# Attention's transposes and weighted values as pairs of 64-row tiles, with later transposes issued ahead

## The reference, cut to what matters

```python
# B=8 sequences of S=64 tokens, D=512, H=16 heads of HD=32, LK=1601 context rows
q = split(hidden @ q_w.T + q_b); k = split(context @ k_w.T + k_b); v = split(context @ v_w.T + v_b)
scores = einsum('bhqd,bhkd->bhqk', q, k) / sqrt(HD)
probs  = softmax(where(mask > 0, -inf, scores))
ctx    = einsum('bhqk,bhkd->bhqd', probs, v)        # weighted values
x = x + ctx ...  # then x + attn(layernorm(x)), x + experts(layernorm(x))
```

## Time and profile before

| what | value |
|---|---|
| median of 3 runs (lowest, highest) | 1251.3 us (1250.09, 1251.83) |
| span of the profiled execution, the time that the profile has of it | 1248.0 us |
| what lies between that span and the runs' median | 3.3 us |
| busy share of PE, DVE, ACT, POOL | 98%, 68%, 54%, 12% |
| mean granted TensorE clock | 0.999 of 2.4 GHz |
| one round of attention | 54.57 us, 16 times |

### The profile page before, as it was taken

How to read it: one execution, slowest core, us unless ns; L and a number is a source line. 1 busy time by engine, 2 the same in 40 slices (tenths; PEclk the granted TensorE clock), 3 DMA queues, 4 the chain that set the end, 5 groups by cost and what they waited for, 6 DMA issues and landing times.

```text
span 1248.0 us, 22257 instructions
## 1 busy us (share of the span) xinstructions
PE 1226.0 (98%) x8533; PEld 1150.7 (92%) x8533; DVE 844.3 (68%) x2213; ACT 676.0 (54%) x1202; POOL 147.5 (12%) x84
## 2 busy tenths in 40 slices
PE   7999999999999999999999999999999999999998
PEld 7899999999999999999999999999978889989996
DVE  6566656566665656666565666677689888877887
ACT  6455545645554564555456355435555666767673
POOL 0003101300310150031013003100012000000012
PEclk9999999999999999999999999999999999999999
DMA  8102200220220022022002202200326777777663
GB/s 297 38 1 91 82 2 1 99 73 1 91 82 1 1 97 76 1 91 81 2 1 99 74 1 91 96 2 1 109 71 240 259 235 269 235 245 259 228 220 129
DMA packets 61046, 126.97 MB, mean 102 GB/s; under 512 B 3644, under 2 KB 21192, under 8 KB 60824
## 3 DMA queue, kind: packets, MB, share of 16 engines
q1 hardware_dynamic: 58776, 118.97, 27.8%
q0 software_dynamic: 2176, 6.72, 1.6%
HBM read 120.01 MB, written 14.32 MB: 108 GB/s over the span
## 4 chain that ended last, share of the span: by engine, by line
PE 88%; DVE 7%; ACT 2%; issue 1%; DMA 1%; SPq 0%; ACTq 0%; DVEq 0%
PE ptp L877 25%; PE work L877 21%; PE pv L1033 7%; PE ptp L1017 7%; PE work L915 7%; PE work L1248 6%; PE work L1250 3%; PE ptp L1271 2%; PE ptp L1274 2%; PE ptp L1272 2%; PE ptp L1273 2%; PE ptp L1275 2%; DVE w_lo L1618 1%; PE work L884 1%; DVE w_lo L1624 1%; DVE pt L1530 1%
## 5 line engine op out<-in xcount | busy, mean ns | idle before, releaser
L877 PE MATMUL ptp<-vw_hi,cx_hi 128*128 128x256 f32 x832 | 241.8, 291 | 0.0
L877 PE MATMUL ptp<-vw_lo,cx_hi 128*128 128x256 f32 x832 | 235.4, 283 | 0.0
L877 PE MATMUL ptp<-vw_hi,cx_lo 128*128 128x256 f32 x832 | 235.3, 283 | 0.0
L540 POOL TENSOR_TENSOR cx_lo<-raw,cx_hi 128x1664 fp32r<-128x1664 f32 x28 | 106.3, 3795 | 669.9 <-ACT cx_hi L601 669.9
L877 PE MATMUL work<-cx_hi,kw_hi 128*128 128x400 f32 (+1 forms) x504 | 175.1, 347 | 0.8 <-DVE cx_lo L1432 0.7
L877 PEld LDWEIGHTS ptp<-vw_hi,cx_hi 128*128 128x128 f32 x832 | 159.2, 191 | 17.0 <-issue 17.0
L877 PE MATMUL work<-cx_hi,kw_lo 128*128 128x400 f32 (+1 forms) x504 | 173.7, 345 | 0.0
L877 PE MATMUL work<-cx_lo,kw_hi 128*128 128x400 f32 (+1 forms) x504 | 173.2, 344 | 0.0
L1530 DVE TENSOR_TENSOR pt<-ptp,pt 128x512 fp32r<-128x512 f32 (+1 forms) x224 | 141.0, 649 | 33.8 <-ACT pt L601 30.3
L877 PEld LDWEIGHTS ptp<-vw_hi,cx_lo 128*128 128x128 f32 x832 | 159.3, 191 | 0.0
L877 PEld LDWEIGHTS ptp<-vw_lo,cx_hi 128*128 128x128 f32 x832 | 159.2, 191 | 0.0
(11 more groups left out here) (291 smaller groups left out, 2371.8 us busy)
## 6 DMA issues: line engine op xcount, KB each, us to landing
w1raw<-in_w SPq DMA_DIRECT2D x32, 1024.0 KB, 5.0
w2raw<-in_w SPq DMA_DIRECT2D x32, 1024.0 KB, 6.2
raw<-in_ctxT SPq DMA_DIRECT2D x31, 832.0 KB, 6.2
pr<-in_mask SPq DMA_DIRECT2D x8, 800.5 KB, 4.3
xrow<-x_rows SPq DMA_DIRECT2D x7, 256.0 KB, 6.1
y_rows<-y_out_rows POOLq DMA_DIRECT2D x7, 256.0 KB, 2.6
xs<-in_x SPq DMA_DIRECT2D x1, 1024.0 KB, 9.2
qwraw<-in_qwT SPq DMA_DIRECT2D x1, 1024.0 KB, 7.8
```

What stands on the lines that cost most here:

```text
L540: pool.tensor_tensor(cx[1][:, :, sl], raw[:, k % 2], cx[0][:, :, sl].bitcast(F32), ALU.subtract).then_inc(c_lo, 1)
L877: last = pe.matmul(dst, lhs(i, c), rhs(j, c), start=(c == 0 and (i, j) == (0, 0)), stop=(c == n - 1 and (i, j) == (1, 0)))
```

## The change

Transposes and weighted values become pairs. Each 128x128 transpose becomes two transposes of 64 rows of probabilities into 64 columns each, in the two row halves of the array, and each writes a bank of its own, so that a block takes a pair of banks. Each 128-row weighted-value product becomes two of 64 context rows, one into bank `ptp2`, one into `pv`, for the same 256 columns; so the sums now lie in two banks, and the sums' end has four copies of 64 rows on ScalarE (L696, L697 before: two), four adds of 64 rows on VectorE (two before) and one add more of 128 x 256.

Eight banks become four pairs: 0 and 1 are the `work` banks 0, 1 and 2, 3; pair 2 is `ptp0` and `ptp1`; pair 3 is `ptp2` and `pv`, where the sums lie while a group is weighed. `PAIR_OF` says which block goes where. Blocks 0 and 1 share pair 3, and both must be read before W0 starts. Step `t` moves from behind k4 to right behind the last scores. In `w0` the order on TensorE is T2 T3 T4 W0 W1 T5 W2 T6 W3 T7 W4 T8 W5 W6, in `w1` T9 T10 W7 T11 W8 T12 W9 T13 W10 W11 W12 W13. T0 waits for v5's bank to be read, T3 and T4 for the last item in work banks 0, 1 and 2, 3 (k1 and k5), T11 for that in 0, 1 (k7), the others for the block that was in their pair. Keys get banks 0, 1, 2, 3, 2, 3 before `w0` and 0, 1 behind it. There are still three slots `pt`. In the last sequence's second round `t` comes behind the last scores too, and the query step moves between `w0` and `w1`; the sum bank of the last group is no longer a `work` bank.

The core of the diff (left out: the same renaming of arguments on ScalarE and VectorE, declarations of banks):

```diff
-        steps += e[2:3] + v[6:] + e[3:]
+        steps += t + e[2:3] + v[6:] + e[3:]
...
-            steps += k[:5]
-        steps += t + k[5:6] + w[:1] + k[6:] + w[1:]
+            steps += k[:6]
+        steps += w[:1] + k[6:] + w[1:]
...
+TURNED_BY = [2, TPH + 2, 2 * TPH]
+FIRST_TURNS = [(2, 3), (TPH + 2, TPH + 3)]
+NEXT_TURN = {0: 4, 2: 5, 3: 6, 4: 7, 5: 8, 8: 11, 9: 12, 10: 13}
+PAIR_OF = [3, 3, 2, 0, 1, 2, 0, 1, 2, 1, 2, 0, 1, 2]
...
+        def turned_block(j, units):
+            jj = j % (2 * TPH)
+            start = 2 * P if jj == 1 else 0
+            return pairs[PAIR_OF[jj]][:, :, start:start + units * S].rearrange("p a (u q) -> p a u q", q=S)
...
-            def fold(b, last, g):
+            def fold(b, g):
                 act.wait_ge(pt_used, NPT * b + TPH * (g + 1) + PTD)
...
-                act.activation(folded[0:2 * HD, :], sums[2 * HD:P, 0:2 * P], ACT.Copy)
-                act.activation(folded[2 * HD:P, :], sums[0:2 * HD, 2 * P:4 * P], ACT.Copy).then_inc(folded_done, 1)
+                act.wait_ge(att_rows, 4 * b + g)
+                for rows, others, cols in sum_parts():
+                    act.activation(folded[rows, 0], sums[0][rows, cols], ACT.Copy)
+                    ins = act.activation(folded[rows, 1], sums[0][others, cols], ACT.Copy)
+                ins.then_inc(folded_done, 1)
...
             def turn(b, last, j):
-                g, first = j // TPH, 2 * (j % TPH)
-                pe.wait_ge(pt_lo, NPT * b + pt_before(j))
-                if j % (2 * TPH) == 0:
-                    pe.wait_ge(w_free, count(b, last, ("v", g // 2, TPH - 1)))
+                g, jj, first = j // TPH, j % (2 * TPH), 2 * (j % TPH)
+                h, pair = g // 2, PAIR_OF[jj]
+                if jj == 0:
+                    pe.wait_ge(w_free, count(b, last, ("v", h, 5)))
+                    pe.wait_ge(pv_free, 4 * b + 2 * h + 1)
+                if jj == 2:
+                    pe.wait_ge(w_free, count(b, last, ("v", h, TPH - 1)))
+                if jj in (3, 4):
+                    pe.wait_ge(w_free, before_pair(b, last, pair, ("w", 2 * h, 0)))
+                elif jj == 11:
+                    pe.wait_ge(w_free, before_pair(b, last, pair, ("w", 2 * h + 1, 0)))
+                elif jj > 4:
+                    owner = max(i for i in range(jj) if PAIR_OF[i] == pair)
+                    pe.wait_ge(pt_lo, NPT * b + 2 * TPH * h + owner + 1 + PTD)
...
-                for n in range(min(2, KT - first)):
-                    for rt in range(2):
-                        ins = pe.transpose(ptp[j % PTD][:, (2 * n + rt) * P:(2 * n + rt + 1) * P],
-                                            pr[:, (2 * g + rt) % 4, (first + n) * P:(first + n + 1) * P], ident[:])
+                for u in range(units):
+                    n, rt = u // 2, u % 2
+                    for a in range(2):
+                        rows = slice(S * a, S * (a + 1))
+                        ins = pe.transpose(block[:, a, u], pr[rows, (2 * g + rt) % 4, (first + n) * P:(first + n + 1) * P],
+                                           ident[rows, rows])
...
-            def weigh(b, last, j):
+            def weigh(b, j):
...
                     for rt in range(2):
-                        ins = pe.matmul(sums[:, rt * 2 * P:(rt + 1) * 2 * P],
-                                         vv[:, kt, g % 2, rt].rearrange("p a d -> p (a d)"),
-                                         pt[:, j % PTD, n, rt].rearrange("p a d -> p (a d)"),
-                                         start=(kt == 0 and rt == 0), stop=(kt == KT - 1 and rt == 1))
+                        for a in range(2):
+                            rows = slice(S * a, S * (a + 1))
+                            ins = pe.matmul(sums[a][:, rt * 2 * P:(rt + 1) * 2 * P],
+                                            vv[rows, kt, g % 2, rt].rearrange("p a d -> p (a d)"),
+                                            pt[rows, j % PTD, n, rt].rearrange("p a d -> p (a d)"),
+                                            start=(kt == 0 and rt == 0), stop=(kt == KT - 1 and rt == 1))
...
             def weighted(b, last, g):
-                end = 2 * TPH * (g // 2 + 1)
-                for j in range(TPH * g, TPH * (g + 1)):
-                    if j + 2 < end:
-                        turn(b, last, j + 2)
-                    weigh(b, last, j)
+                base = 2 * TPH * (g // 2)
+                for jj in FIRST_TURNS[g % 2]:
+                    turn(b, last, base + jj)
+                for jj in range(TPH * (g % 2), TPH * (g % 2 + 1)):
+                    if jj in NEXT_TURN:
+                        turn(b, last, base + NEXT_TURN[jj])
+                    weigh(b, base + jj)
...
             def group_out(b, g):
...
+                for rows, others, cols in sum_parts():
+                    dve.tensor_tensor(folded[rows, 0], sums[1][rows, cols], folded[rows, 0], ALU.add)
+                    ins = dve.tensor_tensor(folded[rows, 1], sums[1][others, cols], folded[rows, 1], ALU.add)
                 ins.then_inc(pv_free, 1)
                 dve.wait_ge(pv_free, 4 * b + g + 2)
+                dve.tensor_tensor(summed, folded[:, 0], folded[:, 1], ALU.add).then_inc(sums_done, 1)
```

More of the change, by code:

```diff
@@ L165, in by_pair, with ring_banks, before_pair @@
     return [bank[:, 0:n * 2 * P].rearrange("p (n g r d) -> p n g r d", n=n, g=2, r=2)[:, :, :, rt, :] for rt in range(2)]
+def ring_banks(last):
+    banks, scored, others, late = [], 0, 0, False
+    for kind, a, j in STEPS[last]:
+        if kind == "s":
+            banks.append(scored % 4)
+            scored, others, late = scored + 1, 0, False
+        elif kind == "w":
+            others, late = 0, True
+        elif kind in "kanq":
+            plain = others % 4 if others < 4 or last else 2 + others % 2
+            banks.append(2 if last and (kind, j) == ("k", 5) else plain)
+            others += 1
+    return banks
+BANKS = [ring_banks(False), ring_banks(True)]
 def bank_of(last, step):
-    return step[2] % PTD if spare(step) else RING[last].index(step) % 4
+    return step[2] % PTD if spare(step) else BANKS[last][RING[last].index(step)]
 def before_bank(b, last, step):
     q = RING[last].index(step)
[L176 to L180, removed]
+    bank = BANKS[last][q]
+    mine = [m for m in range(q) if BANKS[last][m] == bank]
+    if mine:
+        return count(b, last, RING[last][mine[-1]])
+    other = max(m for m in range(len(RING[0])) if BANKS[0][m] == bank)
+    return NW * b + FIRST_K + max(ITEMS[0].index(RING[0][other]) + 1 - NW, bank - 3)
+def before_pair(b, last, pair, weighed):
+    earlier = STEPS[last][:STEPS[last].index(weighed)]
+    return count(b, last, [m for m in earlier if m in RING[last] and bank_of(last, m) // 2 == pair][-1])
 def pt_before(j):
@@ L377, in layer, with sum_parts, pt_part @@
         turn_banks = [work[1], work[2], yb[2], work[3]]
-        def sum_bank(last, g):
-            return work[3] if last and g == 3 else pv
+        def sum_parts():
+            halves = [slice(2 * HD * rt, 2 * HD * (rt + 1)) for rt in range(2)]
+            return [(halves[rt], halves[1 - rt], slice(rt * 2 * P, (rt + 1) * 2 * P)) for rt in range(2)]
+        def turned_block(j, units):
+            jj = j % (2 * TPH)
+            start = 2 * P if jj == 1 else 0
+            return pairs[PAIR_OF[jj]][:, :, start:start + units * S].rearrange("p a (u q) -> p a u q", q=S)
+        def pt_part(j, n, part):
+            return pt[:, j % PTD, 0:n, :, part, :].rearrange("p n r (a q) -> p a (n r) q", a=2)
         def scattered(ph, e):
```

73 lines of the change are left out of this document (33 added, 40 removed).

## The result

The changed kernel takes 1274.8 us (median of 4 runs, 1272.97 to 1276.46) against 1250.7 us for the kernel before beside it (1249.95 to 1251.83). The ratio is 1.0193, 95% interval 1.0179 to 1.0208: 1.9% slower. The forecast was 1270.

A forecast was written before the change was run, and what follows sets the result against it. TensorE, busy 98% of the span, was taken as the bound. 12.2 (15 rounds of +0.81) + 2.7 (mask rounds) + 4.5 (last round) = 19.4 us on 1248.0 gives 1267.4, with the median's 3.3 1270.7; forecast 1270, range 1246 to 1290.

The forecast's parts named there:

- the likeliest case: Whole kernel: slower, at 1270 us (its own range 1260 to 1280), through waits for banks; chance 0.57.
- Pairs of products cost one product: Weighted-value products on TensorE: a pair of 64-row products costs 0.12 us, like one 128-row product, no gain.
- A pair of transposes 0.062: Transposes on TensorE: a pair takes 0.062 us, saving 0.046 on each of 52, 2.4 us a round.
- Rival A: Transposes on TensorE don't get cheaper, 0.108 a pair: 17 us more, 1287; chance 0.15.
- Switches of 0.13 and 0.20: TensorE between 128-row and 64-row work: 0.13 us into a transpose, 0.20 back; 0.26 net a round.
- The waits: TensorE waiting for banks: T0 0.46 us, T4 0.94 (starts at 1.75), T6 0.37 (at 4.16), T11 0.75 (at 2.09).
- Rival B: T0, T4 and T11 find v5's, k5's and k7's banks free: no waits, about 1233 us; chance 0.2.
- Mask rounds: Seven rounds where VectorE converts the mask before the first scores: 0.39 us later each, +2.7 us.
- Rounds together: 15 rounds at +0.81 us (t +0.07, w0 +0.62, w1 +0.12), +12.2, plus 2.7 for rounds with a mask.
- The last round: Last sums, delayed by longer sums, row weights and query copy, ready at 912.6 instead of 908.1: +4.5 us.
- The step from span to runs: Whole kernel: the runs' median lies 3.3 us above the profiled span; carried along, 1267.4 becomes 1270.7.
- Rival C: Whole kernel: switches dearer or cheaper and waits half as long cancel, within 0.2% of before; chance 0.08.

The follow-up runs named there:

- the kernel with paired transposes alone: The changed kernel with only the transposes as 64-row pairs, products of 128 rows into one bank with short sums: 1283.2 us, ratio 1.0259 to the kernel before.
- all three later: The changed kernel with T4 behind W1, T11 behind W8 (T12 behind W9, T13 behind W10) and step t behind v6: 1257.2 us, ratio 1.0055.
- with the row weights moved: T4, T11 and t placed later in the changed kernel, plus last-round row weights behind the last turned blocks instead of the query copy: 1254.9 us, ratio 1.0035.
- the last pair of kernels: Sums handed over in halves and mask converted ahead of sums, added to the 1254.5 us kernel (rows later) and the 1254.9 us one (without): 1243.6 and 1243.3 us.
- the last kernel: The 1254.9 us kernel (turns later, row weights moved, without rows later) plus sums handed over in halves and mask ahead of sums: 1243.3 us, ratio 0.994.
- the other order: The changed kernel's own order, with short sums: 64-row tiles with half of the sums left out 1263.1 us, against 128-row tiles 1277.4 us.
- VectorE's rows are moved: The kernel before, with VectorE's four adds into the attention rows of a half's first group behind the second group's last block: 1250.9 us, ratio 1.000.
- whole tiles: The changed kernel's order, banks and waits, but transposes and products of 128 rows again and short sums: 1277.4 us, ratio 1.0213 to the kernel before.

## Why the prediction was right, and by how much it was off

*Direction and cause* were right, and it was the likeliest case that came. Point by point:

- *Pairs of products cost one product.* Eight products take 0.71 and sixteen 1.19, so a pair is (1.19 - 0.71) / 4 = 0.12: right.
- *A pair of transposes 0.062.* T0 and T1 together (sixteen) take 0.71, eight take 0.46: 0.0625 a pair. Rival A is out.
- *Switches of 0.13 and 0.20.* Two of them cost 0.28 in the kernel with paired transposes alone, where 0.33 was taken. The size is about right; which of the two is the dearer, that kernel does not tell.
- *The waits.* T0 0.41 (scores end 510.93, T0 at 511.34; forecast 0.46), T4 at 1.70 (1.75), T6 at 4.17 (4.16), T11 at 2.06 (2.09). Rival B, that these banks are free in time, is out: VectorE is idle for 1.57 us before k5's subtract, and T4 still starts 1.70 after k5's last product. w0 +0.68 (forecast +0.62), w1 +0.17 (+0.12).
- *Mask rounds.* 0.41 more than the others (0.39).
- *Rounds together.* 17.1 us, with the start's 0.6 apart, against 14.9 forecast. 0.11 a round is missing (1.7 in 15 rounds), which is the 0.06 of w0's term and the 0.05 of w1's; 0.3 more is the one mask round of 56.19, and the last 0.2 I did not follow.
- *The last round* is the term that was mis-sized: +4.5 forecast, 5.9 + 1.7 found. The chain was as described: T11 waits for the query copy behind sums and row weights (2.24), the last sums need 4.95 from W13's end (926.83, where a query product starts) to 931.78 (forecast 4.9). What I left out is the clock. Of the 3.1 us by which the term is short, T11 to W13's end is 1.0 and the query products are 1.7, both in slower stretches; the prediction had put the clock at nothing without a word.
- *The step from span to runs.* I carried 3.3 us from the profiled execution's span to the median. Every execution whose span is on record lies 1.7 to 1.9 above it; the rest of the 3.3 was that the profiled one was a fast one. After the change the median lies 0.2 above the profile's span, since its own execution (1276.46) was the slowest of the four. By the spans the change costs 26.6, by the medians 24.1; forecast 19.4. That the forecast comes within 4.7 of the median, and not within 7.2 as its 1267.4 does of the span of 1274.6, is luck.

Rival C, cancellation to within 0.2%, did not come either. Nearest to it are the kernels with the order mended: all three later is +0.55%, with the row weights moved +0.35%.

What the prediction did not see is how much of the loss could be had back. It had the longer sums in three of its terms (T11's later bank in w1, the mask rounds, the last round) but never added up their share. Without them 11.7 us are gone, nearly half of the loss; and the last pair of kernels, with the longer sums in place, is faster than the kernel before.

**Left open.** Whether the gain of the last kernel (7.4 us) belongs to the tiles: neither its order with 128-row tiles was run, nor the kernel before with its sums handed over in halves and its mask ahead of them. For the tiles speaks that in the other order they save 14.3 us with the sums kept short, that the kernel before has only 0.17 of wait in a round to lose and no longer rounds behind a mask, and that it gains nothing when VectorE's rows are moved. The two edits of the last pair, halves and mask, were run only together. Four slots for turned probabilities instead of three, which might free the last wait of w1 (0.25), were not tried.

## What to carry to other kernels

Before an instruction is issued earlier, look up when the bank that it writes is handed back, and count from the last product into that bank: here product, copy and subtract take 1.6 us, even with VectorE idle, and everything behind the early instruction on TensorE pays. Where a change splits an accumulation into two banks, the reader of these banks gets the bill; look for work of that engine that can stand where it waits anyway, and signal the copies in halves (the two together won 9.0 us by the spans, 11.5 by the medians). And before mixing tile heights inside a loop of short products, price the switches: here two for each block cost 0.28 us, twice what the cheaper transposes saved.

## What the runs showed that I had not expected

**The clock falls behind waits of the last round, and not in every execution.** Besides the trace after, most of the traces of kernels with 64-row products have one or two slower stretches, all in the last round; two have none. The same wait comes with both: 1.85 us for the copy of the hidden rows. The stretches around and behind it in the kernel with all three later and the row weights moved, where T4's products start at 890.57 (columns as above):

```profile
889.00:892.00 3.00, 1.70 (x32) 1.57 (x32) 2.38 (x5) 2.98 (x6) 0.00 (x0) 1.00 0.26 42
892.00:895.00 3.00, 2.73 (x55) 2.52 (x54) 2.39 (x5) 1.86 (x4) 0.00 (x0) 1.00 0.28 53
```

And in the last kernel, where they start at 881.80:

```profile
880.00:883.00 3.00, 1.47 (x22) 1.48 (x24) 2.38 (x5) 2.93 (x6) 0.00 (x0) 0.88 0.28 51
883.00:886.00 3.00, 3.00 (x42) 3.00 (x40) 1.74 (x3) 1.52 (x3) 0.00 (x0) 0.55 0.19 47
```

In the second the sixteen products behind the wait take 1.68 instead of 1.19, and the eight transposes 0.63 instead of 0.40. The same work up to the first group's last products takes 5.24 (881.80 to 887.04) instead of 4.38 (890.57 to 894.95), so this stretch costs 0.9 us on top of the wait. Waits of 0.7 to 1.0 us inside the rounds never did this: the stretches 0 to 860 us of the trace after have a granted clock of 1.00. The traces of the kernel before and of those with whole tiles or with paired transposes alone show no such stretch. They have no wait above 0.82 in the last round; but the one with paired transposes alone has the same 0.69 and 0.73 one behind the other that came ahead of the first stretch after the change. And the tiles are not shown to be the condition: an execution of the kernel with whole tiles that has no trace had a mean clock of 0.997. The clock also goes with the scatter of the times: the nine executions of the kernel with the row weights moved run from 1252.2 us at a mean clock of 0.999 to 1257.7 at 0.996. What decides whether a stretch comes, no run here shows.

**A switch of tile height has a price that short products feel.** The Trainium skill, TensorEngine Tiling (Array Packing), "Key Properties", says that a change of tiling mode drains TensorE, without a figure; the trace agrees that a change costs time, 0.28 us for two, but does not show the drain itself.

**Loads of 64 rows overlap more.** The groups by shape have the weight loads of these transposes (busy us, mean ns | idle before), first in the kernel before, then after:

```profile
L1017 PEld LDWEIGHTS ptp<-ident,pr 128*128 128x128 f32 x832 | 97.5, 140 | 2.6 <-issue 0.7
...
L1077 PEld LDWEIGHTS work<-ident,pr 64*128 64x128 f32 x832 | 36.1, 138 | 38.9 <-DVE kk_lo L1474 24.8 <-DVE pt L1593 6.5 <-issue 3.8
```

A single load is recorded at 140 ns before and 138 after, so it is no shorter. But 832 loads of 128 rows fill 97.5 us together, 117 ns each, and 832 of 64 rows fill 36.1 us, 43 ns each: their records overlap. The two loads of a pair lying side by side do not explain the 0.062 alone. If each load still kept its row half for the time that the rule weighed in the prediction gives, a pair would cost what one transpose cost before; and the experts' transposes of 48 rows start 0.06 apart without a partner in the other half. Whether it is the fewer loaded rows or the 64 moved columns that make the spacing short, no run here separates.
